# A decoder layer on one core: self-attention and cross attention in one program per engine

## The reference

```python
x = layernorm(x + self_attention(x, W_K, W_Q, W_V, W_O))   # 16 heads of 128, causal mask
x = layernorm(x + gamma * cross(x, ctx, ctx))              # see below
x = layernorm(x + ffn(x, W_g, W_u, W_d))                   # quantised x, sign() of the weights, hidden 2048

def cross(q, k, v):            # (B, D, L) read as 8 heads of 64 channels
    qh, kh, vh = [a.reshape(B, 8, 64, 512) for a in (q, k, v)]
    qk = einsum('bhdq,bhdl->bhql', qh, kh) / sqrt(64)
    return einsum('bhql,bhdl->bhdq', softmax(qk), vh).reshape(B, 512, 512)
```

## Time and profile before

| | us |
|---|---|
| median of 3 runs | 1504.88 |
| lowest and highest | 1502.27, 1506.39 |
| the profiled execution, its own time | 1502.57 |
| its span, first to last instruction | 1500.8 |

### The profile page before, as it was taken

The page is one execution under the profiler, slowest core; times in us unless marked ns, Lnnn a source line. Parts: engine busy times, 40 slices in busy tenths (PEclk is TensorE's granted clock), DMA queues, the critical chain, the costliest instruction groups (busy, mean ns, idle before and its releaser), DMA issues. The chain is left out here.

```text
span 1500.8 us, 24088 instructions
## 1 busy us (share of the span) xinstructions
PE 1434.7 (96%) x6988; PEld 1146.6 (76%) x7008; DVE 1100.5 (73%) x2368; ACT 725.1 (48%) x1549; POOL 636.6 (42%) x493
## 2 busy tenths in 40 slices
PE   7999999999999999999999999859999989999996
PEld 5788888888888888888888888737887765565564
DVE  4667677776777676777767776678999995796854
ACT  3444444545444444444353544438987863323332
POOL 1333424334243334242433433357887853343432
PEclk9999999999999999999999999979999999999998
DMA  6566666666656666666666664811224103000000
GB/s 175 155 166 169 167 169 163 167 161 166 161 164 160 161 161 171 167 165 164 162 167 158 168 166 133 210 50 54 60 60 151 36 1 112 1 29 28 0 29 28
DMA packets 193609, 185.09 MB, mean 123 GB/s; under 512 B 97057, under 2 KB 170785, under 8 KB 193313
## 3 DMA queue, kind: packets, MB, share of 16 engines
q1 hardware_dynamic: 192416, 184.09, 45.7%
q10 hardware_dynamic: 1152, 0.52, 0.2%
HBM read 113.25 MB, written 71.30 MB: 123 GB/s over the span
## 5 line engine op out<-in xcount | busy, mean ns | idle before, releaser
L583 ACT ACTIVATE probs<-probs,neg_max 128x128 f32<-128x128 f32 (+3 forms) x256 | 142.5, 557 | 357.8 <-DVE neg_max L707 350.2
L411 POOL TENSOR_TENSOR v_lo<-placed,v_hi 128x512 fp32r<-128x512 f32 x64 | 83.2, 1299 | 366.1 <-ACT v_hi L589 366.1
L413 POOL TENSOR_TENSOR pT_lo<-placed,pT_hi 128x1280 fp32r<-128x1280 f32 x64 | 189.2, 2956 | 0.0
L767 DVE SCALAR_TENSOR_TENSOR acc<-attn_bank,prob_recip,acc 128x512 f32<-128x512 f32 x256 | 174.8, 745 | 8.1 <-PE attn_bank L483 3.3
L1303 POOL TENSOR_TENSOR prod_lo<-prod,prod_hi 128x512 fp32r<-128x512 f32 x64 | 84.7, 1323 | 143.2 <-ACT prod_hi L1412 143.2
L707 DVE CUSTOM_DVE_ANT_0 probs<-attn_bank,mask 128x128 f32<-128x128 f32 (+3 forms) x256 | 117.2, 481 | 8.3
L682 DVE TENSOR_TENSOR qT_lo<-attn_bank,qT_hi 128x512 fp32r<-128x512 f32 x64 | 44.2, 691 | 105.2 <-ACT qT_hi L571 105.2
L950 POOL TENSOR_SCALAR xprobs<-xprobs,xprob_recip 128x512 f32<-128x512 f32 x128 | 99.9, 797 | 36.1 <-DVE xprob_recip L1130 36.0
L719 DVE STREAM_TRANSPOSE turned<-probs 128x256 f32<-128x256 f32 (+1 forms) x384 | 113.9, 362 | 0.0
L1362 PE MATMUL y_bank<-wdT_f32r,prod_hi 128*128 128x512 f32 x256 | 110.7, 432 | 2.3 <-POOL prod_lo L1303 1.8
L483 PE MATMUL attn_bank<-woT_hi,zT_hi 128*128 128x512 f32 x256 | 101.2, 395 | 8.9 <-DVE zT_lo L682 8.9
(11 more groups left out here) (145 smaller groups left out, 3887.5 us busy)
## 6 DMA issues: line engine op xcount, KB each, us to landing
turned_scratch<-turned SPq DMA_DIRECT2D x64, 896.0 KB, 3.9
placed<-turned_scratch SPq DMA_DIRECT2D x256, 224.0 KB, 4.3
rows_twice<-in_ctx_dram SPq DMA_DIRECT2D x64, 128.0 KB, 2.6
acc<-in_x_dram SPq DMA_DIRECT2D x16, 256.0 KB, 5.2
rows<-in_L_attn_W_V_dram SPq DMA_DIRECT2D x64, 64.0 KB, 2.3
rows<-in_L_attn_W_O_dram SPq DMA_DIRECT2D x64, 64.0 KB, 2.7
rows_twice<-in_L_ffn_W_g_dram SPq DMA_DIRECT2D x64, 64.0 KB, 3.1
rows_twice<-in_L_ffn_W_u_dram SPq DMA_DIRECT2D x64, 64.0 KB, 2.0
```

What stands on the lines that cost most here:

```text
L413: nc.gpsimd.tensor_tensor(pT[par][1][:], placed_probs, pT[par][0][:].bitcast(F32), ALU.subtract).then_inc(p_lo, 1)
L583: nc.scalar.activation(probs[:, cols], probs[:, cols], ACT.Exp, bias=low[:, par, t:t + 1], scale=-1.0, accum_out=total[:, par, t:t + 1]).t ...
L767: nc.vector.scalar_tensor_tensor(out=acc[:, b * NT + t, :], in0=s_bank[t][:], scalar=recip[:, b, t:t + 1], in1=acc[:, b * NT + t, :], op0= ...
```

## The change

1. *One block for both attentions.* `attention` and `cross_attention` return functions per engine (`Programs`), and the block calls self-attention's and then cross attention's on each engine. No barrier stands between them. The making of constants moves to the start of GpSimd's program in the same block.
2. *A map of SBUF.* Large tiles have addresses given by hand (`Plan.at`, in KiB from a base), so that tiles of both stages overlay each other where their lives allow. PSUM is eight banks that all stages share. Some buffers are doubled for the last items: `placed` and `zT` have a second one.
3. *Cross attention's beginning inside items 61 to 63.* `CrossBegin` holds functions that self-attention's programs call: the value transposes, the hi and lo halves, the clearing of `val`, the first queries, score units 0 to 7, the first row maxima. The step -1 is gone; `begin_*` stand in its place, and all four batches are written out.
4. *The order of the last four items.* TensorE does output product 61 before value product 62, and waits for `o_added` tile by tile.
5. *Context halves made in self-attention.* Per head one tile of the context is loaded, scaled by 1/8, split by GpSimd (`split`) and kept in DRAM; cross attention loads both halves (`load_halves`) instead of splitting. Of the FFN weights, wu is loaded one item later, since it shares a tile with this.
6. *Queries.* Per pair of heads ScalarE copies the whole tile (`queries_hi`), GpSimd subtracts (`queries_lo`), and SP moves the halves to their places by DMAs from SBUF to SBUF (`load_queries`).
7. *Norm 1.* Batch 0 is normalised by VectorE (first tile) and GpSimd (the others), batch 1 by GpSimd in cross attention's beginning, batches 2 and 3 by GpSimd in items 6 and 7 of batches 0 and 1, with statistics on VectorE at units 2, 9, 16 and 23 (each of batches 0 and 1).
8. *Signs* are loaded in 8 parts, one in each item of batch 2. The FFN's wd has four semaphores, one for each four tiles, instead of sixteen.
9. ScalarE does one small copy right after its first DMA issues, before its first real work.

The diff, without the change of indentation:

```diff
+  def load_split_tile(self, sp, n):
+    sp.dma_start(self.pair[:, 1, :], self.tiles[:, bass.ds(n, 1), :].rearrange("p o d -> p (o d)")).then_inc(self.split_loaded, 16)
+  def split(self, nc, pool, halves, k, n):
+    raw = self.pair[:, 1, :]
+    if not isinstance(n, int) or n > 0:
+      pool.wait_ge(self.halves_kept, n * 16)
+    wait_apart(pool, k, self.split_loaded, n * 16 + 16)
+    nc.gpsimd.tensor_scalar(raw, raw, XSCALE, 1.0, ALU.mult, ALU.mult).then_inc(self.scaled, 1)
+    wait_apart(pool, k, self.scaled, n + 1)
+    nc.gpsimd.tensor_scalar(halves[:, 0, :], raw, 1.0, 1.0, ALU.mult, ALU.mult).then_inc(self.split_hi, 1)
+    wait_apart(pool, k, self.split_hi, n + 1)
+    nc.gpsimd.tensor_tensor(halves[:, 1, :], raw, halves[:, 0, :].bitcast(F32), ALU.subtract).then_inc(self.split_done, 1)
+  def keep_halves(self, sp, halves, k, n):
+    wait_apart(sp, k, self.split_done, n + 2)
+    sp.dma_start(self.kept_tiles[:, bass.ds(n, 1), :, :].rearrange("p o k d -> p (o k) d"), halves[:].bitcast(F32)).then_inc(self.halves_kept, 16)
+  def load_halves(self, sp, cp, b, h):
+    for side in range(2):
+      sp.dma_start(cp[h % 2][side * XD:(side + 1) * XD, :, :].bitcast(F32),
+            self.kept[bass.ds(b, 1), h * XD:(h + 1) * XD, :, :].rearrange("o r k d -> (o r) k d")).then_inc(self.halves_loaded[h % 2], 16)
...
+  def load_part(self, sp, n):
+    c, half = n // 2, slice(n % 2 * HID // 2, (n % 2 + 1) * HID // 2)
     for out, x in ((self.gT, self.gu[0]), (self.uT, self.gu[1])):
-      sp.dma_start(out[:], x).then_inc(self.loaded, 16)
+      sp.dma_start(out[:, c, half], x[:, c, half]).then_inc(self.loaded, 16)
...
+  zT = [halves_of("zT", 96, 2, [P, S]), halves_of("zT_last", 88, 2, [P, S])]
...
+  placed = [plan.at("placed", 112, [P, E, SLAB]), plan.at("placed_last", 76, [P, E, SLAB])]
...
+    def exchange(i, par, loads=None, landing=0):
       sp.wait_ge(p_turn, i + 1)
...
       sp.wait_ge(written, i * 16 + 16)
-      if not isinstance(i, int) or i > 0:
+      if landing:
+        sp.wait_ge(w_lo["wo"], H)
+      elif not isinstance(i, int):
         sp.wait_ge(p_lo, i)
+      elif i > 0:
+        sp.wait_ge(p_lo, min(i, FIRST + 2))
       for c in range(E):
-        sp.dma_start(placed[c * R:(c + 1) * R, :, :],
+        sp.dma_start(placed[landing][c * R:(c + 1) * R, :, :],
...
+      if b == 1:
+        wait_apart(sp, k, rows.split_done, h + 1)
         load_gate_up(sp, "wu", h)
...
         keep_signs(h, 0)
+        wait_apart(sp, k, f_turn, h * 3 + 3)
+        rows.load_split_tile(sp, h)
         if more:
...
         keep_signs(h, 2)
+        rows.keep_halves(sp, halves, k, h)
...
+    for t, name in enumerate(("wk", "wq", "wv", "wo")):
+      sp.wait_ge(w_turn[name], H)
+      rows.load_tile(sp, 0, t)
     loads(H - 1, 0, False)
-    exchange(FIRST + 2, 0)
+    exchange(FIRST + 2, 0, landing=1)
+    loads(H - 1, 1, False)
     loads(H - 1, 2, False)
-    keep_signs(H - 1, 0)
     exchange(FIRST + 3, 1)
+    keep_signs(H - 1, 0)
+    sp.wait_ge(v_full, ITEMS)
+    for item in range(2):
+      rows.load_halves(sp, cross.cp, 0, item)
+    sp.wait_ge(f_turn, (H - 1) * 3 + 3)
+    rows.load_split_tile(sp, H - 1)
     for m in (1, 2):
       keep_signs(H - 1, m)
-    for t, name in enumerate(("wk", "wq", "wv", "wo")):
-      sp.wait_ge(w_turn[name], H)
-      rows.load_tile(sp, 0, t)
-    sp.wait_ge(f_turn, H * 3 + 1)
-    for h in range(2):
-      rows.load_twice(sp, 0, h)
     rows.load_gamma(sp)
+    cross.begin_sync(sp)
+    rows.keep_halves(sp, halves, k, H - 1)
+    sp.wait_ge(o_added, H * B * NT)
...
+    make_constants(nc, pool, k)
     for name in ("wk", "wq", "wv"):
...
         weight_lo("wq", h + 2)
+      if b == 3:
+        rows.split(nc, pool, halves, k, h)
     with pool.Fori(0, H - 1) as h:
...
     weight_lo("wo", H)
-    for b in range(1, B):
-      halves_lo(FIRST + b, b % 2)
-    for b in range(2):
-      norm_gpsimd(nc, pool, norm, k.minus_half, b)
-  @block.tensor
-  def _(pe):
+    halves_lo(FIRST + 1, 1)
+    pool.wait_ge(v_full, ITEMS)
+    cross.clear_values(pool)
+    halves_lo(FIRST + 2, 0, 1)
+    norm_gpsimd(nc, pool, norm, k.minus_half, 0)
+    halves_lo(FIRST + 3, 1)
+    pool.wait_ge(norm.rstd_ready, 1)
+    for t in range(1, NT):
+      cross.apply_norm(pool, 0, t)
+    rows.split(nc, pool, halves, k, H - 1)
+    pool.wait_ge(rows.split_done, H + 1)
+    cross.begin_gpsimd(pool)
...
+    def output_product(i, second=0):
       pe.wait_ge(z_lo, i + 2)
       for t in range(NT):
+        if isinstance(i, int) and i > FIRST:
+          pe.wait_ge(o_added, (i - 1) * NT + (t + 1))
         for n, (zp, wp) in enumerate(SPLIT):
-          last_mm = nc.tensor.matmul(s_bank[t][:], zT[zp][:, t * P:(t + 1) * P], wT["wo"][wp][:],
+          last_mm = nc.tensor.matmul(s_bank[t][:], zT[second][zp][:, t * P:(t + 1) * P], wT["wo"][wp][:],
...
-    output_product(FIRST)
+    output_product(FIRST, 0)
+    output_product(FIRST + 1, 1)
     values_product(FIRST + 2, 2, Z_BANK[2])
-    pe.wait_ge(o_added, FIRST * NT + NT)
-    output_product(FIRST + 1)
-    pe.wait_ge(o_added, FIRST * NT + 2 * NT)
-    output_product(FIRST + 2)
+    pe.wait_ge(v_turn, ITEMS)
+    for pair in range(2):
+      cross.transpose_values(pe, pair)
+    output_product(FIRST + 2, 0)
+    for pair in range(2, 4):
+      cross.transpose_values(pe, pair)
     values_product(FIRST + 3, 3, Z_BANK[3])
-    pe.wait_ge(o_added, FIRST * NT + 3 * NT)
-    output_product(FIRST + 3)
...
+    for unit in range(2):
+      cross.scores(pe, unit)
+    output_product(FIRST + 3, 1)
+    for unit in range(2, 8):
+      cross.scores(pe, unit)
+    pe.wait_ge(o_added, H * B * NT)
+    cross.begin_tensor(pe)
...
     load_projection(act, "wk", wk, 0)
+    act.wait_ge(k.cleared, 1)
+    nc.scalar.copy(k.unused[:, 15:16], k.ones[:, 0:1])
     load_projection(act, "wq", wq, 0)
...
     z_hi_of(0)
-    halves_hi(FIRST + 2, 0)
-    sign(H - 1, 1)
+    halves_hi(FIRST + 2, 0, 1)
     z_hi_of(1)
+    sign(H - 1, 1)
     sign(H - 1, 2)
-    z_hi_of(2)
     halves_hi(FIRST + 3, 1)
+    z_hi_of(2)
+    for pair in range(2):
+      cross.values_hi(act, pair)
+    cross.first_queries_hi(act)
+    for pair in range(2, 4):
+      cross.values_hi(act, pair)
     z_hi_of(3)
-  @block.vector
-  def _(dve):
+    cross.begin_scalar(act)
...
     rows_of_scores(FIRST + 3, 3)
-    z_lo_of(0)
     turn_probs(FIRST + 3, 1)
+    z_lo_of(0)
     turn_ffn("wu", H - 1, 1)
-    add_outputs(FIRST, 0)
     z_lo_of(1)
+    add_outputs(FIRST, 0)
     turn_ffn("wd", H - 1, 2)
-    stats(0)
+    dve.wait_ge(o_added, (FIRST + 1) * NT)
+    norm_stats(nc, dve, k, norm, norm_tiles(acc, 0), LN_EPS, 0, first=True)
     add_outputs(FIRST + 1, 1)
     z_lo_of(2)
-    apply(0)
+    for pair in range(2):
+      cross.values_lo(dve, pair)
+    cross.first_queries_lo(dve)
+    for pair in range(2, 4):
+      cross.values_lo(dve, pair)
     add_outputs(FIRST + 2, 2)
-    stats(1)
     z_lo_of(3)
-    apply(1)
+    for unit in range(2):
+      cross.row_max(dve, unit)
     add_outputs(FIRST + 3, 3)
-    dve.wait_ge(norm.done, B - 2)
-    dve.wait_ge(o_added, H * B * NT)
...
+    cross.begin_vector(dve)
...
+  def load_queries(sp, b, h):
+    rows = slice(h % 2 * XD, (h % 2 + 1) * XD)
+    if h % 2 == 0:
+      wait_apart(sp, k, x_lo, b * PAIRS + h // 2)
+    for part in range(2):
+      sp.dma_start(xs[h % 2][part * XD:(part + 1) * XD, :].bitcast(F32),
+            x_parts[rows, part, :]).then_inc(xs_loaded[h % 2], 16)
+  def begin_sync(sp):
+    for t in range(NT):
+      sp.wait_ge(vt_full, t + 1)
+      source.load_tile(sp, 1, t)
+    for h in (2, 3):
+      sp.wait_ge(scores_full, (h - 1) * NT)
+      load_item(sp, 0, h)
+      load_queries(sp, 0, h)
...
+      if exists(m + 4, ITEMS):
+        nb, nh = ahead(b, h, 4)
+        wait_apart(sp, k, scores_full, m * NT + 3 * NT)
+        load_item(sp, nb, nh)
+        load_queries(sp, nb, nh)
       if is_item(b, h, B - 2, 0):
-        signs.load(sp)
+        sp.wait_ge(signs.kept, H * 48 + 1)
+      if b == B - 2:
+        signs.load_part(sp, h)
...
+  def apply_norm(pool, b, t):
+    tile = tile_of(b, t)
+    nc.gpsimd.tensor_scalar(tile, tile, norm1.mv[:, t, 0:1], norm1.rstd[:, t:t + 1], ALU.subtract, ALU.mult).then_inc(applied, 1)
+  def queries_lo(pool, b, pair):
+    wait_apart(pool, k, x_hi, b * PAIRS + pair)
+    nc.gpsimd.tensor_tensor(x_parts[:, 1, :].bitcast(F32R), tile_of(b, pair), x_parts[:, 0, :], ALU.subtract).then_inc(x_lo, 1)
+  def normalise(pool, m, q):
+    wait_apart(pool, k, recip_ready, m + 1)
+    for t in range(NT):
+      nc.gpsimd.tensor_scalar(probs[q][:, t, :], probs[q][:, t, :], recip[:, q, t:t + 1], 1.0,
+                  ALU.mult, ALU.mult).then_inc(probs_ready, 1)
+  def begin_gpsimd(pool):
+    queries_lo(pool, 0, 1)
+    normalise(pool, 0, 0)
+    normalise(pool, 1, 1)
+    norm_gpsimd(nc, pool, norm1, k.minus_half, 1)
+    pool.wait_ge(norm1.rstd_ready, 2)
+    for t in range(NT):
+      apply_norm(pool, 1, t)
...
```

(92 more changed lines are left out.)

1614 lines of the change are left out of this document (804 added, 810 removed).

## The result

| | before | after |
|---|---|---|
| median of 4 runs | 1503.93 us | 1493.74 us |
| lowest and highest | 1502.27, 1506.39 | 1490.54, 1496.47 |
| span of the profiled execution | 1500.8 us | 1494.7 us |

The ratio is 0.993, with an interval of 0.9917 to 0.9944: faster by 10.2 us, where I forecast 26 to 27. The profiled execution of after is its slowest (1496.47); by the spans it gains 6.1 us.

What follows compares the result with a forecast made beforehand. TensorE, busy 96% of the span, was taken as the bound, with about 35 us of waits and half clock between the attentions. -2.2 - 20.0 - 4.2 - 3.5 + 2.8 = -27.1 gave 1475.5 profiled, forecast 1478 us; range 1466 to 1494.

Steps and rivals of the forecast that it cites:

- Seven norm tiles at 0.8: Around cross attention's beginning: GpSimd's norm tiles priced at 0.8 us each.
- "+2.8" for batch 0's start: Cross attention's first items: query data and normalise(2) late, at 1007 against 1005, with half clock; +2.8 us, bounds 0 and +8.
- the steady items' 0: Cross attention's steady items: GpSimd loses 1.9 us of split per item, gains 1.3 per two; 0, at most +2.8.
- "-4.2" for batch 2: Cross attention, batch 2: norm1's apply goes to GpSimd, statistics spread earlier; four items 31.2 to 27 us, bounds 0 and -4.4.
- the passage: Self-attention's end to cross attention's first value product: new schedule removes waits and half clock; -20.0 us, bounds -23 and -10.
- batch 3's five: Cross attention, five slow items of batch 3: VectorE loses 4 xs_lo and its applies ease; -3.5 us, bounds 0 and -6.
- Step 4: Passage schedule: item 63's slab lands near 968, halves 970, values 63 to 977, score units 0 and 1 to 978.
- Rival A: The passage keeps its waits: gain 11 instead of 20 us, item 16 another 1 late, 1488; chance 0.15.
- D: The passage stays as long; only the start and batches 2 and 3 gain: 1498, up to 1502; chance 0.04.
- The start: Kernel's beginning: SP's first DMA no longer waits for the constants; -2.2 us, bounds 0 and -3.1.
- Rival B: Cross attention's queries: new DMA route makes items wait from a landing of 5.6 us; 1523 at 7.2; chance 0.05.
- Rival C: Whole passage: GpSimd blocks VectorE's two-SBUF-input operations through their shared port pair; +8 us, 1486; chance 0.06.

Runs made afterwards that it cites:

- e5: After, with GpSimd's norm tile leaving out the subtraction of the mean (measurement only): 1478.07 us, ratio 0.9824.
- e6: After, with GpSimd's norm tile written as add and mult with the negated mean, whole norm computed: 1476.83 us, ratio 0.9821.
- e2: After, with the slow norm tiles spread, one in every second item of the batch before, and the variance at unit 30: 1474.53 us, ratio 0.9803.
- e13: e9 with batch 0's four context tiles loaded only in 16 of 512 columns (measurement only): 1469.92 us, ratio 0.9781.
- e14: Before, with only the making of constants moved into self-attention's block: 1501.15 us, ratio 0.9984.
- e1: After, with VectorE's wait for GpSimd's last norm tile moved from ahead of the statistics to ahead of the variance: 1493.70 us.
- e10: e9 with item 63's slab written ahead of the load of wd, and wd and the context tiles issued during that write: 1472.18 us, ratio 0.9791.
- e9: After with add/mult norm tiles, spread singly, and ScalarE's z_hi of item 62 ahead of the halves of item 63's slab: 1472.54 us, ratio 0.9799.
- e4: After, plus a measurement of nine forms of a 128x512 elementwise instruction on GpSimd, in two places; no kernel time given.

## Why the prediction was wrong

1. **GpSimd's norm tile: the step that failed.** "Seven norm tiles at 0.8", and with it the apply of batches 1 to 3. I took the price from the earlier trace rows, L950: a tensor_scalar on GpSimd, same shape, same two-operation form, 0.796 us. But L950 is mult with mult, and the tile is subtract with mult: 2.07. The trace of before had no GpSimd subtract in a tensor_scalar, so this was a price that I had not seen, and I gave the price no upper bound. With 2.07, batch 1's four tiles end at 1012.4, and SP sends for the query halves behind them at 1013.7, where I had these landed at 1007. The "+2.8" for batch 0's start became +8.3 (item 1; its bound was +8), the steady items' 0 became +4.3 (item 9), and "-4.2" for batch 2 became +0.2 (2.9 + 1.3 lost in items 17 and 18). That is 16.8 us of stalls, and e5 and e6 gave back 15.7 and 16.9. It is luck that this is also what the medians miss against the forecast (27.1 - 10.2 = 16.9): without the stalls the start of batch 0 costs 0 and not +2.8, and the passage, at -17 in most kernels, lacks about 3 of its -20. The two misses cancel. The measured 1493.74 lies inside my range (1466 to 1494) by luck too: the terms named with its upper end, passage -10 and batch 0 +5, add up to 1490 only, and those of its lower end to 1469.
2. **Bursts.** My argument that GpSimd loses 1.9 us per item and has room holds for the mean (14.4 to 16.2 us busy in each 20 with the spread tiles, 1000 to 1120 in e2), not for four tiles in one go: normalise is only two items ahead, and e2 shows it with the price unchanged.
3. **Batch 2 and 3 otherwise right.** With e2's tiles items 16 to 19 take 27.0 us, as forecast; batch 3's five took 34.8 in after (forecast 35.5, -4.1 for -3.5). Cross attention without the stalls is 211.7 (e2): -7.3, against my -4.9, or -7.7 without the +2.8.
4. **The passage** came to -14.6 in the profile, -17 in most kernels, against -20. Its order and its gaps were as worked out (output product 61 ahead of value product 62, the last gap for zT_last_lo). What I left out is the 1 MB of context tiles, costed as four issues on SP: 2.9 us (e13). Step 4 had item 63's slab near 968; in the old trace's time v_hi starts on it at 971.3 in e6 and at 968.3 in e13. The further 2.4 us that after's own profile lacks are open. Rival A, the waits that stay, holds in part (one gap of 4.79 us, and half rate behind it); D doesn't.
5. **The start**: -2.2 forecast, -2.4 to -2.7 by e14; right.
6. **Rival B**: xs and cp (3.6 and 3.9 us from issue to landing) make no steady item wait; the threshold of 5.6 wasn't reached. **Rival C**, the port: GpSimd's tile is as slow with VectorE still, and VectorE's usual operations didn't change (row maximum 683 and 682 ns, xpT_lo 685 and 684, before and after). What changed is small: VectorE's one norm tile of the passage took 1.02 us, where it takes 0.48 with GpSimd still. And the 0.796 of L950 was a mean: its median is 0.693 and its longest 1.152, and in after the same operation has a mean of 0.703. In before the group of four at 1042.03 took 3.12 us beside one of VectorE's xs operations (1041.88), which the change took away; that they hinder each other fits this, and no run tests it.
7. The loop: TensorE busy 100.00 of 100, x490, as before.

## What to carry over

An operation that moves to another engine keeps its name and not its price: same instruction, same shape and same number of operands as a row of the trace is not enough when the ALU operations differ. Measure the very pair beforehand: no row of this shape in the trace would have served as an upper bound either, as the dearest GpSimd group in before took 1.32 us. When an in-order engine stalls, try its cure before believing the wait that the trace names: removing the longest wait (e1) gained nothing, spreading or cheapening the work behind it gained 17 to 19 us. Transfers moved into a stretch where DMAs feed the critical chain cost here their bytes, in whatever order they were issued; issuing the critical one earlier only made it take longer (e10).

The fastest versions that compute the whole layer are e9 and e10, 1472.54 and 1472.18 us, 31 us under before and 21 under after. Their 2 us over e2 (1474.53) are not shown to come from their edits, as the passage is the same.

## What the runs showed of the hardware

- GpSimd's tensor_scalar on 128x512 float32: 0.77 us for mult/mult, mult/add and add/mult with two pointers, and mult/mult 0.70 with one and 0.62 with none; 1.57 for a lone subtract; 1.93 to 2.08 for every other pair tried (subtract/mult, mult/subtract, add/add, subtract/subtract, max/mult, mult/min). The price of subtract/mult was the same beside a busy VectorE (e2); of most others it was taken with VectorE still. On 128x128 0.45 and 0.79.
- The same tile on VectorE is 0.48 with GpSimd still, so the move cost a factor of 4.3, and the cheap form 1.6.
- tensor_tensor subtract on GpSimd, 128x512, with the same float32 tile as both inputs: 1.04 (e4). With two different tiles it was longer: the addition into `acc` took 1.29 in after, also float32.
- The DMAs of one slab, first issue to first reader: 6.8 us in e6, 6.5 with 1 MB less in flight (e13), 11.9 when they went out 2.9 us earlier, beside the loads moved behind the slab's write (e10).
